# Graph attention on one core: one-hot matrices by ScalarE and VectorE instead of by matrix products, and another order of the gathers' holds

## The chip, the core and the metric

The kernel runs on one core of a Trainium2 chip. The metric is the device time of one execution in microseconds; a smaller one is better. Traces come from the hardware profiler, from one execution on the same core.

## The reference, cut to what matters

There are 6250 nodes of 128 features, 200000 edges sorted by destination (`dst`), with random sources (`src`) and 64 edge features, and 8 heads of 16.

```python
q = (x @ Wq + bq).reshape(N, 8, 16); k = ...Wk...; v = ...Wv...
scores = jnp.sum(q[dst] * k[src], axis=-1) * 16 ** -0.5 + (edge_attr @ We + be)
e = jnp.exp(scores - jax.ops.segment_max(scores, dst, N)[dst])
denom = jax.ops.segment_sum(e, dst, N) + 1e-10
agg = jax.ops.segment_sum((e / denom[dst])[:, :, None] * v[src], dst, N)
out = layernorm(x + agg.reshape(N, 128) @ Wo + bo)
```

All is float32. The number of nodes in a stretch of edges is small, since the edges are sorted: a half block of edges touches at most 64 nodes in a row.

## The kernel before, in words

**Tiling.** A tile is 128 edges. The edges are cut into 57 blocks (`b`). A full block has two halves of 14 tiles, 28 tiles; each half touches at most 64 nodes, so a block's 128 partitions hold 64 nodes of each half. A block is worked in 7 steps (`q`) of 4 tiles (2 pairs); 391 of the steps are full. The program is written out in full, without loops, as a list of slots (`v`): slot v works on step v, 7 slots a block. Each engine runs its own list in order and waits on semaphores.

**Prologue.** Rows of keys and values of all nodes are computed and stored as `kv_table` in device memory. The first block's are computed from gathered rows of x.

**A step.** GpSimd gathers the key and value rows of 4 tiles, one indirect DMA a tile (L523), into `kv_buf`, which holds three blocks. TensorE spreads the block's queries to edges: `spread_q` (L1230) multiplies a one-hot matrix (node by edge) with `q_blk` into one of two banks `ps_q`. VectorE multiplies with the keys (`multiply`, L850) and adds up by head (`dot`, L860). 12 slots later (SLOT + LAG) the weights are there; VectorE multiplies the values with them (`weigh`, L870) into one of two buffers `wv`, ScalarE copies the weights beside them (`copy_weights`, L655), and one slot after that TensorE adds them up by node with a one-hot matrix (edge by node): `sum_step` (L1266).

**One-hot matrices.** In slot v TensorE's `match(v)` (L1210, L1216) computes both matrices for later use: that by node of step v+1 and that by edge of step v-12, as products of bfloat16 codes. The code of an edge is made of its relative destination d, that of a node of its number n, so that the product is -(n-d)^2 or, for equal ones, 0. ScalarE's `copy_hots(v)` (L613, L617) takes relu(1 + product), which is 1 or 0, from the bank `ps_t` into one of two buffers `hots`. `match(v)` waits for the copy of slot v-1, `spread_q(v)` and `sum_step(v)` for that copy too, and `copy_hots(v)` for `match(v)`, the spread of v-1 and the sums of slot v-2. The edge codes are computed in the prologue by ScalarE from `dst_row`, stored to `code_table`, and loaded by block, 2 x 10.5 KB, by SP (`load_codes`).

**Once a block** TensorE also signals ten things: left-over row, maxima crossing edges, edge terms, edge terms turned, carried row summed, ends turned, new queries, halves folded, aggregate turned, rows times Wo. So it signals 7 + 7 + 7 + 10 = 31 times a full block. Of these, VectorE waits for the fold (`add_folded`), the left-over row (`scale_carry`), the ends turned (`crossing_maxima`, L930) and the crossing maxima (`edge_maxima`), and TensorE waits for VectorE's answers in the slots beside them.

**The order around the change.** In a slot TensorE's list is: spread, match, sums, then what is once a block. VectorE's is: weigh, multiply, the block's maxima, dot, the block's end. ScalarE's is: copy_hots, exponentials, copies for the block's end, copy_weights. SP's list is by block: edges of b+1 (1024 KB), x of b+3, codes of b+1, end distances of b+1, then the store of block b-3, for which it waits longest.

**The holds.** GpSimd could run far ahead. From block 6 on (`HELD`) step q's gathers are held to the work two steps behind (`AHEAD`):

```python
if b >= HELD and t == t0:     pool.wait_ge(s_byedge, q - AHEAD + 1)
if b >= HELD and t == t0 + 1: pool.wait_ge(s_matched, HOTS_TO[slot_of(q - AHEAD)])
if b >= HELD and t == t0 + 2: pool.wait_ge(s_summed, q - AHEAD - SLOT - LAG)
```

In full blocks these are TensorE's spread, match and sums of slot q-2, which it does in this order.

## Time and profile before

| what | us |
|---|---|
| median of 3 runs | 2431.14 |
| lowest, highest | 2421.57, 2438.39 |
| span of the profiled execution, its own time | 2449.4 |
| TensorE matmul busy | 1545.6 |
| VectorE busy | 1370.8 |
| ScalarE busy | 454.6 |
| GpSimd busy | 1496.0 |

The span goes from the first to the last instruction of one execution; the profile gives no other time of it. Busy times are the sums over an engine's instructions. Idle time of an engine is put down to what ended it; "issue" is idle time for which the profile shows no cause, "remote" is idle time ended by something it can't name. Ends of matmuls are modelled, not measured.

### The profile page before, as it was taken

The page shows a single profiled execution, that of the slowest core. Times are in us where ns is not written, and L with a number is a line of the kernel's source. Part 1 is how long each engine was busy: PE and PEld are TensorE (multiplying, and loading weights), DVE is VectorE, ACT ScalarE, POOL GpSimd, SP SyncE. Part 2 cuts the span into 40 slices and gives each one's busy share as a digit, 9 for nine tenths or more (in the row PEclk, how much of TensorE's full clock was granted, in tenths as well). Part 3 has the DMA queues.
Part 4 walks back from the last instruction along what each step waited for, and adds up shares of the span by engine and source line. Part 5 has one row for each costly group of instructions (what it writes and reads, how often), then busy time and mean ns, then how long its engine had stood idle before and what let it go on. Part 6 is the DMA issues. An engine that isn't in the chain of part 4 may idle for free.

```text
span 2449.4 us, 25231 instructions
## 1 busy us (share of the span) xinstructions
PE 1545.6 (63%) x6655; PEld 1051.5 (43%) x6655; DVE 1370.8 (56%) x3214; ACT 454.6 (19%) x1496; POOL 1496.0 (61%) x1572
## 2 busy tenths in 40 slices
PE   5354576657665757566656666566766666666566
PEld 4233454435343434444444444344444444444344
DVE  4254575656555655555655656555555555556556
ACT  1011121212121211111111212111211212111112
POOL 4736546666666666666666666666666666666661
PEclk7677788868778777877887887877878778788878
DMA  6423334343334334343434343434334343434331
GB/s 248 160 84 105 94 101 130 107 123 115 118 117 130 109 108 130 107 131 108 129 108 128 111 129 108 128 108 125 112 113 127 110 128 111 126 111 127 108 106 31
DMA packets 115143, 288.11 MB, mean 118 GB/s; under 512 B 45909, under 2 KB 53856, under 8 KB 107960
## 3 DMA queue, kind: packets, MB, share of 16 engines
q0 software_dynamic: 74624, 203.26, 28.3%
q1 hardware_dynamic: 37628, 76.52, 9.4%
q10 hardware_dynamic: 2748, 6.69, 0.7%
q8 instruction: 57, 0.93, 0.2%
q14 instruction: 86, 0.70, 0.1%
HBM read 274.69 MB, written 11.67 MB: 117 GB/s over the span
## 4 chain that ended last, share of the span: by engine, by line
PE 40%; issue 25%; another core or an unknown queue 14%; DVE 10%; POOL 9%; DMA 1%; ACT 1%; DVEq 0%; ACTq 0%; POOLq 0%
PE ps_q L1230 14%; PE ps_a L1266 11%; POOL kv_buf L523 9%; PE ps_e L1242 2%; PE ps_t L1216 2%; PE ps_t L1210 2%; DVE prod L850 1%; DVE score L860 1%; DMA kv_buf<-kv_table,src_i 1%; PE ps_s L1294 1%; DVE wv L870 1%; PE ps_a L1319 1%; DVE run_fwd L912 1%; PE ps_a L1320 1%
## 5 line engine op out<-in xcount | busy, mean ns | idle before, releaser
L523 POOL DMA_INDIRECT kv_buf<-kv_table,src_i x1536 | 1465.6, 954 | 899.6 <-issue 407.5
L1230 PE MATMUL ps_q<-q_blk,hots 128*128 128x256 f32 x1564 | 566.4, 497 | 553.8 <-issue 553.6
L1230 PEld LDWEIGHTS ps_q<-q_blk,hots 128*128 128x128 f32 x1564 | 351.9, 246 | 677.7 <-issue 625.2
L1266 PE MATMUL ps_a<-wv,hots 128*128 128x272 f32 x1564 | 559.9, 490 | 8.5 <-issue 5.6
L613 ACT ACTIVATE hots<-ps_t 128x512 f32<-128x512 f32 x377 | 225.1, 597 | 1784.8 <-remote 1035.1
L850 DVE TENSOR_TENSOR prod<-ps_q,kv_buf 128x512 f32<-128x512 f32 (+1 forms) x392 | 268.7, 685 | 497.8 <-remote 322.7
L870 DVE TENSOR_TENSOR wv<-kv_buf,ps_w 128x512 f32<-128x512 f32 (+1 forms) x392 | 266.3, 679 | 238.8 <-remote 179.5
L1266 PEld LDWEIGHTS ps_a<-wv,hots 128*128 128x128 f32 x1564 | 335.4, 238 | 61.0 <-issue 10.4
L860 DVE TENSOR_REDUCE score<-prod 128x32 f32<-128x512 f32 (+1 forms) x392 | 267.2, 682 | 7.9 <-issue 0.2
L930 DVE TENSOR_TENSOR_SCAN ps_s<-seq_far,seq_left,ps_s 8x512 f32<-8x512 f32 x57 | 72.7, 1275 | 188.0 <-remote 155.0
L1309 PE MATMUL ps_a<-sums_sb,carry_from 128*1 128x136 f32 x112 | 28.0, 342 | 195.2 <-DVE sums_sb L982 154.8
L1216 PE MATMUL ps_t<-node_code,codes 128*128 128x128 bf16 x782 | 127.7, 252 | 1.9 <-ACT hots L617 1.9
L1210 PE MATMUL ps_t<-codes,node_code 128*128 128x256 bf16 (+1 forms) x392 | 128.3, 327 | 0.0
L1216 PEld LDWEIGHTS ps_t<-node_code,codes 128*128 128x128 bf16 x782 | 90.3, 116 | 68.3 <-issue 36.3
L1309 PEld LDWEIGHTS ps_a<-sums_sb,carry_from 128*1 128x1 f32 x112 | 4.8, 81 | 215.4 <-DVE sums_sb L982 170.0
L655 ACT COPY wv<-weight 128x32 f32<-128x32 f32 (+1 forms) x392 | 96.1, 245 | 1.3
L1319 PE MATMUL ps_a<-bias_row,ones 1*128 1x128 f32 x114 | 30.8, 354 | 76.6 <-ACT agg_t L663 75.3
L1210 PEld LDWEIGHTS ps_t<-codes,node_code 128*128 128x128 bf16 x392 | 45.3, 116 | 68.5 <-issue 52.9
L936 DVE TENSOR_TENSOR_SCAN seq_b<-seq_far,ps_s 8x512 f32<-8x512 f32 x57 | 68.3, 1198 | 0.0
L1242 PE MATMUL ps_e<-edge_f,w_e 128*32 128x512 f32 (+1 forms) x456 | 66.7, 660 | 0.0
L1319 PEld LDWEIGHTS ps_a<-bias_row,ones 1*128 1x128 f32 x114 | 18.7, 204 | 99.4 <-ACT agg_t L663 90.8
L982 DVE TENSOR_TENSOR sums_sb<-ps_a,sums_sb 1x136 f32<-1x136 f32 x57 | 16.9, 297 | 63.2 <-remote 60.2
(157 smaller groups left out, 1398.1 us busy)
## 6 DMA issues: line engine op xcount, KB each, us to landing
edge_f<-in_edge_blk SPq DMA_DIRECT2D x55, 1024.0 KB
kv_buf<-kv_table,src_i POOLq DMA_INDIRECT x1536
kv_table<-kv_buf ACTq DMA_DIRECT2D x12, 512.0 KB, 3.2
xt_blk<-in_x_t SPq DMA_DIRECT2D x114, 32.0 KB
out<-y_out SPq DMA_DIRECT2D x114, 32.0 KB
kv_buf<-in_x_perm SPq DMA_DIRECT2D x5, 512.0 KB
codes<-code_table SPq DMA_DIRECT2D x108, 10.5 KB
code_table<-kv_buf SPq DMA_DIRECT2D x1, 1344.0 KB
```

What stands on the lines that cost most here:

```text
L523: pool.indirect_dma_start(kv_buf[:, b % NBUF, t, :], None, kv_table, bass.IndirectOffsetOnAxis(ap=src_i[:, column:column + 1], axis=0)).th ...
L613: one = act.activation(hots[:, v % 2, :, :].rearrange("p k n -> p (k n)"), ps_t[:, :], ACT.Relu, bias=1.0)
L655: act.copy(wv[:, q % 2, 0:t1 - t0, D:WV], by_head(weight[:, b % 2, :], TILES[b])[:, :, t0:t1].rearrange("p h t -> p t h")).then_inc(s_besi ...
L850: dve.tensor_tensor(prod[:, q % 2, 0:n * D].rearrange("p (t d) -> p t d", d=D), ps_q[q % 2][:, 0:n * D].rearrange("p (t d) -> p t d", d=D) ...
L860: dve.tensor_reduce(score[:, b % 2, :, t0:t1].rearrange("p h t -> p t h"), prod[:, q % 2, 0:(t1 - t0) * D].rearrange("p (t h d) -> p t h d ...
L870: dve.tensor_tensor(wv[:, q % 2, 0:t1 - t0, 0:D].rearrange("p t (h d) -> p t h d", d=HD), kv_buf[:, b % NBUF, t0:t1, D:KV].rearrange("p t ...
L1210: one = pe.matmul(ps_t[:, 0:(t1 - t0) * W], node_code[:, :], codes[:, b % CBUF, t0 * W:t1 * W], start=True, stop=True)
L1216: one = pe.matmul(ps_t[:, QUAD * W + k * P:QUAD * W + (k + 1) * P], codes[:, b % CBUF, t0 * W + k * P:t0 * W + (k + 1) * P], node_code[:, ...
L1230: one = pe.matmul(ps_q[q % 2][:, k * 2 * D:(k + 1) * 2 * D], hots[:, (v - 1) % 2, 0, k * P:(k + 1) * P], q_blk[:, b % QBUF, :], start=True ...
L1242: one = pe.matmul(ps_e[at:at + P // EGROUPS, 0:n * P].rearrange("k (s p) -> k s p", p=P), w_e2[:, :], edge_f[:, b % 2, :].rearrange("k (s ...
L1266: one = pe.matmul(sums(b), hots[:, (v - 1) % 2, 1, k * P:(k + 1) * P], wv[:, q % 2, 2 * k:2 * k + 2, :].rearrange("p j w -> p (j w)"), sta ...
L1319: pe.matmul(projected(b), ones[0:1, :], bias_row[:, QKV:QKV + D], start=True, stop=False)
```

## The change

`match`, the codes, their table and their set-up go. The matrices come from elsewhere:

- By node, on ScalarE: SP loads the destinations of block b+1 as int32, each half's row repeated over 64 partitions (`load_dst`, 2 x 448 KB a block, two buffers). In slot v ScalarE computes |d - n| for step v+3 (`gaps_to_nodes`) and relu(1 - that) for step v+2 (`hots_by_node`), each 128x256, into four buffers.
- By edge, on VectorE: `hots_by_edge` compares the numbers 0 to 63 with each edge's relative destination, 128x256, ahead of `weigh`, into three buffers.
- `ps_t` becomes a third bank for the spread (`SPREADS`); `wv` has three buffers.
- The gathers from block 6 on wait for other signals. The wait for `weigh` of three blocks before stays only before block 6.

```diff
+    NHOT, NGAP, EHOT, WVBUF, SPREADS = 4, 3, 3, 3, 3
...
-            def load_codes(b):
-                if b >= CBUF:
-                    last = (b - CBUF) * SLOT + GS[b - CBUF] - 1
-                    sync.wait_ge(s_matched, HOTS_TO[last + SLOT + LAG])
+            def load_dst(b):
+                if b >= DBUF:
+                    sync.wait_ge(s_gap, FIRST[b - DBUF + 1])
                 n = HALF[b] * P
                 for j in range(2):
                     row = 2 * b + j
+                    sync.dma_start(dst_bc[j * W:(j + 1) * W, b % DBUF, 0:n], dst_row[row:row + 1, 0:n].to_broadcast([W, n])
+                                   ).then_inc(s_dstbc[b % DBUF], 16)
...
-                    if b >= NBUF:
+                    if NBUF <= b < HELD:
                         pool.wait_ge(s_weighted, steps_over(b - NBUF, t1))
...
                         if b >= HELD and t == t0:
+                            pool.wait_ge(s_summed, q - AHEAD - SLOT - LAG)
+                        if b >= HELD and t == t0 + 1:
                             pool.wait_ge(s_byedge, q - AHEAD + 1)
-                        if b >= HELD and t == t0 + 1:
-                            pool.wait_ge(s_matched, HOTS_TO[slot_of(q - AHEAD)])
-                        if b >= HELD and t == t0 + 2:
-                            pool.wait_ge(s_summed, q - AHEAD - SLOT - LAG)
...
+            def gaps_to_nodes(q):
+                b, g = STEPS[q]
+                t0, t1 = STEP[b][g]
+                if g == 0:
+                    act.wait_ge(s_dstbc[b % DBUF], 32 * (b // DBUF + 1))
+                if q >= NGAP:
+                    act.wait_ge(s_near, q - NGAP + 1)
+                act.activation(gaps[:, q % NGAP, 0:(t1 - t0) * W], dst_bc[:, b % DBUF, t0 * W:t1 * W], ACT.Abs,
+                               bias=neg_node[:, b:b + 1]).then_inc(s_gap, 1)
+
+            def hots_by_node(q):
+                b, g = STEPS[q]
+                t0, t1 = STEP[b][g]
+                act.wait_ge(s_gap, q + 1)
+                if q >= NHOT:
+                    act.wait_ge(s_byedge, q - NHOT + 1)
+                act.activation(near_hots[:, q % NHOT, 0:(t1 - t0) * W], gaps[:, q % NGAP, 0:(t1 - t0) * W], ACT.Relu,
+                               bias=1.0, scale=-1.0).then_inc(s_near, 1)
...
-                copy_hots(-1)
-                for v in SLOTS:
-                    if v in HOTS_TO:
-                        copy_hots(v)
+                act.wait_ge(s_node, NODE["of blocks"])
+                for v in range(-3, SLOTS[-1]):
+                    if step_in(v + 3) is not None:
+                        gaps_to_nodes(step_in(v + 3))
+                    if step_in(v + 2) is not None:
+                        hots_by_node(step_in(v + 2))
...
-            dve.memset(codes[:, :, :].rearrange("p i e -> p (i e)").bitcast(F32), ONES_BF16).then_inc(s_const, 1)
...
+            def hots_by_edge(q):
+                b, g = STEPS[q]
+                t0, t1 = STEP[b][g]
+                pairs = (t1 - t0) // 2
+                if q >= EHOT:
+                    dve.wait_ge(s_summed, q - EHOT + 1)
+                dve.tensor_tensor(
+                    edge_hots[:, q % EHOT, 0:pairs * P].rearrange("p (k j n) -> p k j n", j=2, n=W),
+                    iota_n[:, 0:W].rearrange("p (a b n) -> p a b n", a=1, b=1).to_broadcast([P, pairs, 2, W]),
+                    rel[:, columns(b, 0, TILES[b])].rearrange("p (j t a) -> p t j a", j=2, a=1)[:, t0 // 2:t1 // 2]
+                    .to_broadcast([P, pairs, 2, W]), ALU.is_equal)
...
                     if step_in(v - SLOT - LAG) is not None:
+                        hots_by_edge(step_in(v - SLOT - LAG))
                         weigh(step_in(v - SLOT - LAG))
...
-            def match(v):
...
             def spread_q(v):
                 pe.wait_ge(s_qcopied, b + 1)
-                pe.wait_ge(s_copied, HOTS_TO[v - 1])
-                if q >= 2:
-                    pe.wait_ge(s_product, q - 1)
+                pe.wait_ge(s_near, q + 1)
+                if q >= SPREADS:
+                    pe.wait_ge(s_product, q - SPREADS + 1)
...
-                    if v in HOTS_TO:
-                        match(v)
```

`weigh` and `copy_weights` now wait for the sums of three steps before where it was two, and `sum_step` reads `edge_hots` and the third `wv`.

## Rows read from the trace of the kernel before

**Rows 1.** The page, busy time, share of the span and instructions of each engine.
```profile
PE 1545.6 (63%) x6655; PEld 1051.5 (43%) x6655; DVE 1370.8 (56%) x3214; ACT 454.6 (19%) x1496; POOL 1496.0 (61%) x1572
```

**Rows 2.** Stretches: length; busy us (records) of PE, PEld, DVE, ACT, POOL; clock, DMA share, GB/s.
```profile
283.00:352.00 69.00, 47.46 (x232) 33.38 (x230) 48.77 (x113) 15.78 (x52) 29.55 (x31) 0.84 0.31 93
1057.00:2349.00 1292.00, 830.96 (x3566) 562.25 (x3566) 733.13 (x1708) 243.42 (x807) 827.22 (x868) 0.79 0.39 117
```

**Rows 3.** Groups by line, 1057 to 2349 us, GpSimd: busy, mean ns, idle before.
```profile
L523 POOL DMA_INDIRECT kv_buf<-kv_table,src_i x868 | 828.0, 954 | 465.1 <-issue 229.4 <-remote 168.9 <-PE ps_q L1230 50.5
```

**Rows 4.** Timeline, 1196.5 to 1207.4 us: start, length, engine, line, [idle before].
```profile
1197.62 0.28 PE L1216 MATMUL ps_t<-node_code,codes 128*128 128x128 bf16 x2
...
1197.73 1.14 PE L1266 MATMUL ps_a<-wv,hots 128*128 128x272 f32 x4
...
1203.44 0.95 POOL L523 DMA_INDIRECT kv_buf<-kv_table,src_i  x1 [0.30 <-issue]
...
1206.66 0.60 ACT L613 ACTIVATE hots<-ps_t 128x512 f32<-128x512 f32 x1 [10.69 <-remote]
1206.80 0.69 DVE L870 TENSOR_TENSOR wv<-kv_buf,ps_w 128x512 f32<-128x512 f32 x1 [2.76 <-remote]
1206.89 0.95 POOL L523 DMA_INDIRECT kv_buf<-kv_table,src_i  x1 [2.51 <-remote]
...
1207.35 0.77 PE L1230 MATMUL ps_q<-q_blk,hots 128*128 128x256 f32 x1 [8.49 <-issue]
```

**Rows 5.** Waits, 1057 to 2349 us: who, for what: us, times, longest.
```profile
ACT hots L613 <- remote: 636.8, 82, 13.2
...
PE ps_q L1230 <- issue: 310.7, 69, 10.7
ACT hots L613 <- PE ps_t L1216: 253.4, 88, 8.5
...
DVE prod L850 <- remote: 190.5, 52, 8.5
POOL kv_buf L523 <- remote: 168.9, 86, 3.2
...
DVE ps_s L930 <- remote: 101.6, 19, 8.8
...
POOL kv_buf L523 <- PE ps_q L1230: 50.5, 52, 2.7
...
POOL kv_buf L523 <- PE ps_a L1266: 11.8, 11, 2.3
```

**Rows 6.** Groups by line, whole span, from L613 on with forms kept apart.
```profile
L1210 PE MATMUL ps_t<-codes,node_code 128*128 128x256 bf16 (+1 forms) x392 | 128.3, 327 | 0.0
L1216 PE MATMUL ps_t<-node_code,codes 128*128 128x128 bf16 x782 | 127.7, 252 | 1.9 <-ACT hots L617 1.9
...
L613 ACT ACTIVATE hots<-ps_t 128x512 f32<-128x512 f32 x377 | 225.1, 597 | 1784.8 <-remote 1035.1 <-PE ps_t L1216 499.3 <-issue 219.1
L617 ACT ACTIVATE hots<-ps_t 128x256 f32<-128x256 f32 x26 | 9.9, 383 | 76.8 <-issue 29.6 <-PE ps_t L1210 18.2 <-remote 15.1
L584 ACT ACTIVATE kv_buf<-kv_buf,run_max 128x1792 bf16<-128x1792 int32 x1 | 1.8, 1788 | 0.0
...
L850 DVE TENSOR_TENSOR prod<-ps_q,kv_buf 128x512 f32<-128x512 f32 x390 | 267.8, 687 | 497.6 <-remote 322.7 <-PE ps_q L1230 110.2 <-issue 60.4
...
L736 DVE MEMSET codes<- 128x3584 f32 x1 | 3.0, 3045 | 0.7 <-issue 0.7
```

**Rows 7.** The chain of waits, 1270 to 1292 us: start, length, what.
```profile
1287.28 2.51 DMA kv_buf<-kv_table,src_i
```

**Rows 8.** A stretch with an edge load, columns as in rows 2.
```profile
1208.00:1213.00 5.00, 3.60 (x13) 2.18 (x11) 3.43 (x9) 0.73 (x2) 3.94 (x4) 0.73 0.89 311
```

**Rows 9.** One line's instructions: shortest, median, longest ns, first and last start.
```profile
L523 POOL DMA_INDIRECT kv_buf<-kv_table,src_i x1536: 941/947/1846, 63.8 to 2404.8; - x192
...
L957 DVE TENSOR_TENSOR run_max<-run_max,cand x57: 242/391/455, 165.8 to 2427.5; 128x224 f32<-128x224 f32 x54, 128x208 f32<-128x208 f32 x1, 128x128 f32<-128x128 f32 x1, 128x80 f32<-128x80 f32 x1
```

More of the change, by code:

```diff
@@ L89, in graph_attention @@
     FIRST_HALVES = [(g, h) for g in range(GS[0]) for h in range(2)]
-    assert all(t1 - t0 == QUAD for t0, t1 in STEP[0]) and NB >= 4 and len(GROUPS) >= KNOWN
+    assert all(t1 - t0 == QUAD for t0, t1 in STEP[0]) and NB >= 4
     HALVES_TO = [sum(1 for j, _ in HALVES if j < k) for k in range(len(GROUPS) + 1)]
@@ L275, in graph_attention @@
         SETUP = numbered("ident zero", "iotas", "ident")
-        s_rowcode = sem("s_rowcode")
-        ROWCODE = numbered("less", "rel", "middle", "squares")
-        s_nodecode = sem("s_nodecode")
-        NODECODE = numbered("numbers", "squares", "high", "columns", "rows")
+        s_node = sem("s_node")
+        NODE = numbered("numbers", "of blocks")
         s_const = sem("s_const")
-        CONST = numbered("ones", "zeros", "codes", "iota", "bias kv", "scaled")
+        CONST = numbered("ones", "zeros", "iota", "bias kv", "scaled")
         s_win = sem("s_win")
@@ L429, in _ @@
                 load_x(b)
-            sync.wait_ge(s_const, CONST["codes"])
-            sync.wait_ge(s_codetable, 16)
-            load_codes(0)
+            load_dst(0)
             for i in range(STAGES):
@@ L474, in _ @@
                     if b + 1 < NB:
-                        load_codes(b + 1)
+                        load_dst(b + 1)
                         load_seq(b + 1)
@@ L727, in _ @@
             dve.memset(eps_c[:, :], LN_EPS)
-            for k, less in enumerate((0.0, -32.0, -16.0)):
-                dve.memset(less_c[:, k:k + 1], less)
             dve.memset(q_blk[:, :, :], 0.0)
@@ L796, in _ @@
             dve.tensor_copy(base_bc[:, :], base_ps).then_inc(s_win, 1)
+            dve.wait_ge(s_node, NODE["numbers"])
+            for j in range(2):
+                own = slice(j * W, (j + 1) * W)
+                one = dve.tensor_scalar(neg_node[own, :], base_ps[own, j::2], -1.0, neg_n[own, :], ALU.mult, ALU.add)
+            one.then_inc(s_node, 1)
             dve.tensor_scalar(carry_from[:, 1::2], step_ps[:, 1::2], part[:, 0:1], None, ALU.is_equal)
@@ L1265, in sum_step @@
                 for k in range((t1 - t0) // 2):
-                    one = pe.matmul(sums(b), hots[:, (v - 1) % 2, 1, k * P:(k + 1) * P],
-                                    wv[:, q % 2, 2 * k:2 * k + 2, :].rearrange("p j w -> p (j w)"),
+                    one = pe.matmul(sums(b), edge_hots[:, q % EHOT, k * P:(k + 1) * P],
+                                    wv[:, q % WVBUF, 2 * k:2 * k + 2, :].rearrange("p j w -> p (j w)"),
                                     start=(t0 + k == 0), stop=False)
@@ L1326, in _ @@
                     project_q(b)
-                match(-1)
                 for v in SLOTS:
```

170 lines of the change are left out of this document (36 added, 134 removed).

## The prediction

> **What bounds the kernel now.** I read the shares first: no engine is full. TensorE is busy 63% of the span, GpSimd 61%, VectorE 56%, ScalarE 19% [rows 1]. So the bound is a wait or a ring of waits, and the stretch view says where. In 1057 to 2349 us, 868 gathers were issued, 31 blocks of 28, so a block takes 1292 / 31 = 41.7 us. The earlier stretch 283 to 352 us holds 232 matmul records against 3566 / 31 = 115 a block, two blocks in 69 us, while GpSimd was busy 29.6 us of it [rows 2]. TensorE, ScalarE and VectorE can thus do a block in 34.5 us when GpSimd issues little.
>
> GpSimd's own floor: a gather takes 0.954 us [rows 3] and the next starts 0.30 us later [rows 4], so 28 take 28 x 1.255 = 35.1 us. The block is 6.6 us longer. GpSimd's waits in the stretch say why: 168.9 us end by something unnamed, 50.5 by the spread, 11.8 by the sums, 231 us in 149 pauses, 4.8 a block; without the 0.30 us that stands before any gather it is 186 us, 6.0 a block [rows 5]. GpSimd waits for TensorE.
>
> Why TensorE is late is the point of the case. The records of the matching and sum matmuls end at 1197.9 and 1198.9, yet ScalarE, VectorE and GpSimd, which all wait for exactly these, go on at 1206.66, 1206.80 and 1206.89: three engines released within 0.25 us, eight us later, and 2.3 us after the last of an unbroken row of gathers [rows 4]. ScalarE's copy then releases the next spread at 1207.35, where TensorE had shown 8.49 us of "issue". I read it so: **while gathers are issued back to back, what TensorE finishes is seen late; when GpSimd runs out of leave, all of it comes at once.** The trace doesn't say whether the matmuls or their signals are held.
>
> That makes a ring of signals cost what work does not. Before, spread(v) needs the copy of the hots of v, which needs the matching product of slot v-1, which is behind spread(v-1): one slot per seen signal. In the stretch ScalarE idles 636.8 + 253.4 us before that copy, TensorE 310.7 us before the spread, VectorE 190.5 us before its multiply [rows 5].
>
> **The change, part by part.**
> *Products out.* 391 slots lose one 128x256 and two 128x128 bf16 products, 128.3 + 127.7 = 256 us of TensorE's busy time [rows 6], and 7 of its 31 signals a block (7 spread, 7 matched, 7 summed, 10 once a block). It leaves 24 against 28 gathers. As TensorE is not full, the 256 us are worth nothing as work; what counts is the ring. After, spread(v) needs a hot that ScalarE made two slots before, out of loaded numbers, and the product of v-3; the sum in slot v needs VectorE to be past multiply(v-2). So after one seen signal TensorE can go on for two slots, not one.
> *ScalarE.* It loses a 597 ns copy and gets two operations on 256 columns. The 256-column copy took 383 ns, the 1792-column one from int32 1788 [rows 6]; I take 0.4 us each, 0.8 for 0.6, +80 us busy, to 22%. Cover: it works two and three slots ahead. If that goes (a load of destinations late in slot 4, where the first gap of the next block stands ahead of the exponentials), the sums are late next.
> *VectorE.* 391 comparisons, 128x256. Between 391 ns at 224 columns [rows 9] and 687 at 512 [rows 6] lie 1.03 ns a column, so 0.425 us, 166 us in all: 3.0 us a block on 23.7 (733.1 / 31 [rows 2]). They stand before weigh and multiply. Covered in the slots where VectorE waits for TensorE or gathers anyway; naked in the two slots a block where fold, left-over row and turned ends go back and forth. So 0 to 166 us; I take 2 x 0.425 x 54 = 45 us.
> *Banks.* The freed bank lets spread run three ahead; a third wv buffer lets weigh and the weights' copy wait for sums one step older. No cost; in the gain of the ring.
> *Holds.* In slot v TensorE does spread, then sums, and signals in this order. The first gather of step v+2 used to go with spread(v), the second with the match, the rest with the sums. Now all four wait for the sums, and the second's wait for the spread is always met already: one wait, not two. Behind it only gathers queue. Cost: the first gather starts later by one to two signals. The landing after a last gather took 2.51 us [rows 7], so the data of step v+2 is there 5.0 + 2.5 = 7.5 us after the sums of v, and is wanted two slots, 10 us or more, later. Bounds: 0, or one pause a step (below). I take 0.
> *Loads.* Codes of 2 x 10.5 KB a block are replaced by 2 x 448 KB of destinations spread over partitions. The nearest row is the edge load of 1024 KB: in the 5 us around it the DMA engines are 0.89 busy [rows 8], against 0.39 on the whole [rows 2], 2.5 us more than usual. So 0 to 2.2 us a block, 126 us if every burst delayed a gather that is waited for; I take 0, since the edge burst didn't stop GpSimd (3.94 of 5 us busy) and these loads are issued four slots before their use. SP's queue: load_dst stands where load_codes stood, behind load_x, and its wait is over a slot or more before.
> *Set-up.* The code rows, their store and a memset of 3.0 us [rows 6] go: 0 to 6 us; I take 3.
>
> **The sum.** Between nothing and all of the 6.6 us I take half, 3.3: the ring's reach doubles, so a pause is needed half as often for it, while the ten block signals stay. 51 held blocks x 3.3 = 168; 168 - 45 + 3 = 126 us less. Against the profiled span of 2449.4, 2323. That span stands 18 us above the median of the runs, 2431.1, so **2305**.
>
> **A rule against the change.** The edge comparison is a two-input operation out of SBUF, issued while gathers run. The trace has such: a 224-column one of VectorE has a median of 391 and at most 455 ns, and over 1536 gathers the shortest is 941 and the median 947 [rows 9]. So neither holds the other by any amount that shows, and by these rows the comparison costs GpSimd nothing. The Trainium skill (SBUF — State Buffer, "Who interferes with whom") says that a VectorE instruction with two SBUF inputs contends with a GpSimd instruction that reads SBUF, and that whoever is first holds the other off wholly; by that rule the sum would be that of rival (e), 2471.
>
> **Rivals.**
> (a) *Floor reached*: the pauses vanish and GpSimd issues without a break: 2449 - 51 x 6.6 - 18 = 2095. For it: the 34.5 us of rows 2 and fewer signals than gathers. Against it: those two blocks had a half-idle GpSimd; the ten block signals still go round.
> (b) *Nothing moves*: the turned ends (101.6 us of waiting [rows 5]) and the other once-a-block exchanges take what the ring gives back: 2431, within 1%.
> (c) *Slower, a pause a step.* Place: GpSimd before a step's first gather. With the leave given in one piece after the sums, every step may run into a pause; the unnamed ones took 168.9 / 86 = 1.96 us, 1.66 without the gap. Seven a block make 35.1 + 11.6 = 46.7 us, 5.0 more: 2431 + 255 = 2686. It decides from 6.0 / 1.66 = 3.6 such pauses a block upward. For it: GpSimd can no longer slip one gather per signal. Against it: sums now come second, not third, behind fewer signals.
> (d) *Slower, the comparison in VectorE's path*, with no gain beside it: 2431 + 166 = 2597. Against it: VectorE idles 18 of 41.7 us a block.
> (e) *Slower, gathers held*: each of the 391 comparisons holds a gather for its own 0.425 us. GpSimd's floor grows by 3.0 us a block, 166 in all: 2305 + 166 = 2471. Against it: rows 9.
>
> **Chances.** Forecast 0.46, its own range 2200 to 2400; (a) 0.13; (b) 0.13; (c) 0.13; (d) 0.09; (e) 0.06. A measurement here tells about 1% from no change. Faster 0.59, same 0.13, slower 0.28. Leaving out the fast half of (a) and most of (c), the range is 2140 to 2590.
>
> **What would show it.** Right: the mean time of a block in the steady stretch near 38.5 us, GpSimd's waits for TensorE near 3 us a block, TensorE's idle time before spreads well under 310.7 us, VectorE 27 us busy a block, gathers still 0.95 us. Wrong: pauses before a step's first gather in most steps (c); GpSimd waiting while VectorE shows no idle time (d); gathers over 1 us (e); ScalarE waiting for loaded destinations. It fails if TensorE's results are late for another reason than gathers, so that two slots of reach pass no faster than one.

## The result, and the profile after

| kernel | median us | lowest, highest | runs |
|---|---|---|---|
| before | 2430.14 | 2421.57, 2438.39 | 4 |
| changed | 2401.8 | 2400.68, 2406.15 | 4 |

The ratio is 0.9886, with a 95% interval of 0.9862 to 0.991: 28 us faster, where 126 were forecast. The direction was right and the time is inside the whole range of the forecast (2140 to 2590), just outside the 2200 to 2400 that the forecast gave its own case; the size was off by a factor of four and a half. The profiled execution of before has a span 19 us above its median, the changed one's 2398.6 us is at its own. So the two spans differ by 50.8 us and the medians by 28.

The page of the changed kernel, busy time of the engines, which answers to [rows 1]:

```profile
PE 1449.8 (60%) x5480; PEld 979.4 (41%) x5480; DVE 1493.1 (62%) x3591; ACT 526.8 (22%) x1868; POOL 1496.5 (62%) x1572
```

TensorE's busy time fell by 96 us, not by the 256 of the removed groups [rows 6]. The modelled spans of matmuls overlap: in the trace of before, the removed groups have only 55 of the 1545.6 us to themselves. So a group's busy time is more than what its removal takes off the engine.

The same stretch as in [rows 2], 1057 to 2349 us, columns as there:

```profile
1057.00:2349.00 1292.00, 782.07 (x2992) 524.30 (x2993) 829.87 (x2000) 292.40 (x1046) 848.39 (x888) 0.76 0.51 141
```

888 gathers for 868: 28 x 1292 / 888 = 40.7 us a block for 41.7. VectorE works 829.9 / 31.7 = 26.2 us a block, close to the 27 forecast. Groups by line of that stretch (first row) and of the whole span (the others), to be held against [rows 3, 6]:

```profile
L487 POOL DMA_INDIRECT kv_buf<-kv_table,src_i x888 | 848.4, 955 | 445.6 <-issue 252.3 <-remote 149.4 <-PE ps_a L1191 38.8
...
L559 ACT ACTIVATE x_first<-dst_bc,neg_node 128x256 f32<-128x256 int32 (+1 forms) x392 | 197.0, 503 | 47.8 <-DMA dst_bc<-in_dst_row 30.4 <-issue 17.3
L807 DVE TENSOR_TENSOR x_first<-iota_n,rel 128x256 f32<-128x256 f32 (+1 forms) x392 | 162.4, 414 | 0.0
L568 ACT ACTIVATE x_first<-x_first 128x256 f32<-128x256 f32 (+1 forms) x392 | 157.8, 403 | 215.8 <-remote 193.4 <-PE ps_q L1156 8.9 <-PE ps_t L1156 8.1
```

A gather is as long as before, 0.955 us. The comparison takes 0.414 us (0.425 taken), ScalarE's two operations 0.503 and 0.403 (0.4 each taken). GpSimd's wait for something unnamed is 149.4 us where it was 168.9, 5.0 us are left of the wait for the spread (50.5 before), and that for the sums went from 11.8 to 38.8.

The waits of the stretch, longest groups, to be held against [rows 5]:

```profile
...
DVE prod L787 <- remote: 210.5, 40, 8.8
...
PE ps_a L1191 <- ACT wv L605: 96.8, 25, 10.8
...
PE ps_a L1204 <- DVE sums_sb L926: 91.8, 16, 8.3
PE ps_a L1234 <- issue: 82.9, 19, 5.7
```

TensorE no longer waits before the spread (310.7 us before). It waits before the sums, 182 us for 2, and before the fold (L1204) and the left-over row (L1234), two once-a-block exchanges with VectorE: 281 us, 8.9 a block, where it waited 93 us, 3.0 a block, before. The same picture as in [rows 4], from the timeline of the changed kernel (start, length, engine, line, idle time before):

```profile
1212.89 1.33 PE L1156 MATMUL ps_q<-q_blk,x_first 128*128 128x256 f32 x4
...
1214.06 1.08 PE L1191 MATMUL ps_a<-wv,x_first 128*128 128x272 f32 x4
...
1216.12 0.95 POOL L487 DMA_INDIRECT kv_buf<-kv_table,src_i  x1 [0.30 <-issue]
1217.89 0.69 DVE L787 TENSOR_TENSOR prod<-ps_q,kv_buf 128x512 f32<-128x512 f32 x1 [6.57 <-remote]
1217.95 0.42 ACT L568 ACTIVATE x_first<-x_first 128x256 f32<-128x256 f32 x1 [6.26 <-remote]
```

The sums end at 1215.1, the row of gathers at 1217.07, and VectorE and ScalarE go on 0.06 us apart at 1217.9, as three engines did before.

**Where the pauses went.** From all gaps between gathers over 0.45 us between 434 and 2300 us (0.30 of each taken off, as the usual gap), sorted by the slot of the step that the gather is held to:

| | gathers | pauses a block | us a block | of it slots 0, 3, 4, 5 | slots 1, 2, 6 | gathers in a row |
|---|---|---|---|---|---|---|
| before | 1255 | 4.15 | 6.41 | 2.66 | 3.75 | 6.7 |
| changed | 1282 | 2.64 | 5.51 | 0.26 | 5.25 | 10.6 |
| before with the changed holds | 1267 | 3.20 | 6.05 | 2.53 | 3.52 | 8.7 |
| changed with holds like the earlier ones | 1253 | 3.53 | 6.14 | 4.42 | 1.72 | 7.9 |

The last two rows are of experiments below. The slots are parted by what the first two rows show. In TensorE's list the sums of slots 1, 2 and 6 come next after once-a-block work: the fold and the left-over row (1), the turned ends and aggregate (2), the carried row and the new queries (6). But slot 3, which has the crossing maxima at its head, lost its pauses (1.31 to 0.09 us a block).

So the pauses of the other slots did vanish (2.4 us a block), and 1.5 of it came back in slots 1, 2 and 6, in fewer and longer pauses; with the holds alike (third row against second) it is 2.3 and 1.7. Where a pause stands also depends on the hold: with the first gather held to the spread, most of them stand in slots 0 and 3, so the split says where GpSimd waits and not by itself why. What remains is 0.9 us a block, 46 us over 51 blocks in this pair of profiles, less 6 us at the end: from the end of the last gather to the end of the span it is 49.7 us for 43.6. Ten comparisons of 0.414 us, 4.1 in all, start in that time; whether they lengthen it is not shown.

### The profile page after: what moved, and what is told of

The parts are those of the page before. It is cut to its first block, busy times and chain, and to the rows that moved or that the text cites. A ratio compares the mean times of both kernels' runs of the same rounds, so it can differ in the third digit from the quotient of the medians.

```text
span 2398.6 us, 23254 instructions
## 1 busy us (share of the span) xinstructions
PE 1449.8 (60%) x5480; PEld 979.4 (41%) x5480; DVE 1493.1 (62%) x3591; ACT 526.8 (22%) x1868; POOL 1496.5 (62%) x1572
## 4 chain that ended last, share of the span: by engine, by line
POOL 32%; another core or an unknown queue 21%; issue 19%; PE 17%; DVE 9%; ACT 2%; DMA 1%; ACTq 0%; DVEq 0%
POOL kv_buf L487 32%; PE ps_a L1191 5%; PE ps_q L1156 4%; DVE prod L787 2%; DVE wv L819 2%; PE ps_t L1156 2%; PE ps_e L1168 1%; DVE score L797 1%; PE ps_a L1234 1%; DVE x_first L807 1%; ACT x_first L559 1%; PE ps_s L1213 1%; DMA kv_buf<-kv_table,src_i 1%; PE ps_s L1219 0%
## 5 line engine op out<-in xcount | busy, mean ns | idle before, releaser
L1191 PE MATMUL ps_a<-wv,x_first 128*128 128x272 f32 x1564 | 571.8, 500 | 325.3 <-ACT wv L605 188.5
L1191 PEld LDWEIGHTS ps_a<-wv,x_first 128*128 128x128 f32 x1564 | 362.3, 242 | 497.1 <-issue 212.1
L787 DVE TENSOR_TENSOR prod<-ps_q,kv_buf 128x512 f32<-128x512 f32 x262 | 179.9, 686 | 472.2 <-remote 296.2
L1156 PE MATMUL ps_q<-q_blk,x_first 128*128 128x256 f32 x1046 | 354.7, 472 | 22.6 <-issue 22.6
L1156 PEld LDWEIGHTS ps_q<-q_blk,x_first 128*128 128x128 f32 x1046 | 234.6, 239 | 79.1 <-issue 40.7
L559 ACT ACTIVATE x_first<-dst_bc,neg_node 128x256 f32<-128x256 int32 (+1 forms) x392 | 197.0, 503 | 47.8 <-DMA dst_bc<-in_dst_row 30.4
L568 ACT ACTIVATE x_first<-x_first 128x256 f32<-128x256 f32 (+1 forms) x392 | 157.8, 403 | 215.8 <-remote 193.4
L1234 PE MATMUL ps_a<-sums_sb,carry_from 128*1 128x136 f32 x112 | 33.7, 402 | 249.5 <-issue 134.2
L1156 PE MATMUL ps_t<-q_blk,x_first 128*128 128x256 f32 x518 | 179.9, 481 | 4.8 <-DVE prod L787 4.3
L613 ACT COPY agg_t<-ps_a 128x128 f32<-128x128 f32 x57 | 15.1, 265 | 672.8 <-issue 266.5
L807 DVE TENSOR_TENSOR x_first<-iota_n,rel 128x256 f32<-128x256 f32 (+1 forms) x392 | 162.4, 414 | 0.0
L1204 PE MATMUL ps_a<-sums_sb,carry_from 64*1 64x136 f32 x114 | 30.9, 365 | 189.8 <-DVE sums_sb L926 141.7
L879 DVE TENSOR_TENSOR_SCAN ps_s<-seq_far,seq_left,ps_s 8x512 f32<-8x512 f32 x57 | 72.6, 1274 | 103.2 <-remote 58.7
L1156 PEld LDWEIGHTS ps_t<-q_blk,x_first 128*128 128x128 f32 x518 | 118.7, 244 | 34.1 <-issue 14.2
L1234 PEld LDWEIGHTS ps_a<-sums_sb,carry_from 128*1 128x1 f32 x112 | 4.8, 81 | 275.3 <-issue 149.2
L1204 PEld LDWEIGHTS ps_a<-sums_sb,carry_from 64*1 64x1 f32 x114 | 4.6, 77 | 219.5 <-DVE sums_sb L926 157.5
L595 ACT ACTIVATE ps_w<-run_fwd 128x112 f32<-128x112 f32 (+3 forms) x114 | 29.4, 258 | 244.8 <-issue 227.2
```

The source lines that it names most:

```text
L559: act.activation(gaps[:, q % NGAP, 0:(t1 - t0) * W], dst_bc[:, b % DBUF, t0 * W:t1 * W], ACT.Abs, bias=neg_node[:, b:b + 1]).then_inc(s_ga ...
L568: act.activation(near_hots[:, q % NHOT, 0:(t1 - t0) * W], gaps[:, q % NGAP, 0:(t1 - t0) * W], ACT.Relu, bias=1.0, scale=-1.0).then_inc(s_n ...
L787: dve.tensor_tensor(prod[:, q % 2, 0:n * D].rearrange("p (t d) -> p t d", d=D), ps_q[q % SPREADS][:, 0:n * D].rearrange("p (t d) -> p t d" ...
L807: dve.tensor_tensor(edge_hots[:, q % EHOT, 0:pairs * P].rearrange("p (k j n) -> p k j n", j=2, n=W), iota_n[:, 0:W].rearrange("p (a b n) - ...
L879: dve.tensor_tensor_scan(turned_ends, far[:, 0:SEQ], turned_ends, left, ALU.add, ALU.max).then_inc(s_seqf, 1)
L1156: one = pe.matmul(ps_q[q % SPREADS][:, k * 2 * D:(k + 1) * 2 * D], near_hots[:, q % NHOT, k * P:(k + 1) * P], q_blk[:, b % QBUF, :], start ...
```

## Two kinds of chips

The experiments met a surprise that belongs ahead of them. The kernel before takes 2430.14, 2433.39, 2431.96 and 2426.88 us on four occasions, and 2022.74, 2021.14 and 2022.43 us on three others. The first are called late chips here, the second prompt chips. No chip on record was used on two occasions, so the chip and the occasion can't be told apart; all comparisons are with the kernel before on the same chip. On a prompt chip both kernels were profiled too. GpSimd's gathers over the whole span, before (first fence) and changed (second):

```profile
L523 POOL DMA_INDIRECT kv_buf<-kv_table,src_i x1536 | 1460.5, 951 | 474.4 <-issue 424.0 <-PE ps_q L1230 38.9 <-DVE wv L870 5.2
```

```profile
L487 POOL DMA_INDIRECT kv_buf<-kv_table,src_i x1536 | 1471.4, 958 | 489.2 <-issue 441.4 <-PE ps_a L1191 30.6 <-PE ps_t L1156 7.9
```

The gather is as long as on the late chip (951 against 954 ns in [rows 3]), and there is no unnamed wait at all. The timeline of the kernel before on the prompt chip, against [rows 4]:

```profile
1201.97 0.28 PE L1216 MATMUL ps_t<-node_code,codes 128*128 128x128 bf16 x2
...
1202.21 0.94 POOL L523 DMA_INDIRECT kv_buf<-kv_table,src_i  x1 [0.30 <-PE ps_q L1230]
...
1202.28 0.60 ACT L613 ACTIVATE hots<-ps_t 128x512 f32<-128x512 f32 x1 [2.19 <-PE ps_t L1216]
```

ScalarE starts 0.03 us after the matching product's end, in the middle of a row of gathers. The trace also records when a semaphore is raised. Each raise on record is set here against the last matmul that raises it and had ended by then (434 to 2300 us; 434 to 1900 on the prompt chip; 434 to 1600 without gathers):

| | late: sums, mean us | late: spread, mean us |
|---|---|---|
| before, late chip | 2.7 | 1.8 |
| changed, late chip | 2.6 | 3.0 |
| before, prompt chip | 0.01 | 0.01 |
| changed, prompt chip | 0.01 | 0.01 |
| changed without gathers, late chip | 0.01 | 0.01 |

TensorE's signals are late only while gathers run and only on late chips. Of these two signals, 70% (before) and 87% (changed) of the raises that are more than 0.3 us late fall into a pause of the gathers, half of those 2.0 and 2.7 us or more after the last gather's end: they come in bursts.

Three things limit this. Raises are missing from the traces of late chips: 251 are there for 314 sums in before's window, 221 for 322 in the changed kernel's, 169 for 314 dot products of VectorE in before's; on the prompt chip each of these is there. The means are of the recorded ones. No run separates the issuing of gathers from their transfers, since without gathers both are gone. And every execution on record was profiled, so that no run shows whether the recording itself, whose records go missing on the same chips, takes part in the lateness. What differs between the chips no run shows.

## The experiments

Letters of theories are explained in each expectation. Each ratio has its 95% interval behind it.

### The new holds and the new matrices, one without the other

The kernel before with the changed holds:

```diff
-                    if b >= NBUF:
+                    q = FIRST[b] + g
+                    if NBUF <= b < HELD:
                         pool.wait_ge(s_weighted, steps_over(b - NBUF, t1))
...
                         if b >= HELD and t == t0:
+                            pool.wait_ge(s_summed, q - AHEAD - SLOT - LAG)
+                        if b >= HELD and t == t0 + 1:
                             pool.wait_ge(s_byedge, q - AHEAD + 1)
-                        if b >= HELD and t == t0 + 1:
-                            pool.wait_ge(s_matched, HOTS_TO[slot_of(q - AHEAD)])
-                        if b >= HELD and t == t0 + 2:
-                            pool.wait_ge(s_summed, q - AHEAD - SLOT - LAG)
```

> The kernel before with nothing but the changed kernel's holds: all four gathers of a held step wait for the sums two steps before. Theory H: pauses of 2.4 us in place of 1.8, 4.3 a block: 2.6 us a block more, 2560 us. Theory V and theory X: the order of the holds does little, 2430 within 20; then the whole of the 28 us comes from the matrices. If it is below 2415, the holds alone brought the gain.

Measured on a prompt chip, for which nothing was forecast: 2035.62 us, 1.006 (1.0039 to 1.0081). Again, for a late chip:

> The kernel before with the changed kernel's holds, once more; where before takes 2021 to 2023 it took 2036. Where before takes about 2430: theory H (the holds gave the gain: one pause for each step instead of three waits): 2395 to 2410. Theory V (the matrices made ahead gave it): 2430 or more, since the sums are still behind the matching product. The matching ring with the later leave: 2560 (from my first expectation).

Measured: 2430.37 us for 2431.96, 0.9996 (0.9963 to 1.0029). On a late chip the holds alone give nothing, and the 2560 of my first expectation was far off. The changed kernel with holds like the earlier ones. There is no match to hold the second gather to, so it waits for nothing of its own:

```diff
-                    if NBUF <= b < HELD:
+                    if b >= NBUF:
                         pool.wait_ge(s_weighted, steps_over(b - NBUF, t1))
...
                         if b >= HELD and t == t0:
+                            pool.wait_ge(s_byedge, q - AHEAD + 1)
+                        if b >= HELD and t == t0 + 2:
                             pool.wait_ge(s_summed, q - AHEAD - SLOT - LAG)
-                        if b >= HELD and t == t0 + 1:
-                            pool.wait_ge(s_byedge, q - AHEAD + 1)
```

> The changed kernel with the holds spread first: a held step's first gather waits for the spread two steps before, its third for the sums (and, as in the kernel before, every step for the weighing of three blocks before, which is long past). Theory H (the gain was eaten by holding all four gathers to the sums, which makes each of GpSimd's 2.6 pauses a block 2.4 us long where the kernel before had 4.3 of 1.8): the pauses get shorter by about 0.6 us, 1.6 us a block, 80 us in all: 2320 us. Theory V (the gain was eaten by VectorE's comparison): no change, 2402 within 10. Theory X (what remains are the exchanges between TensorE and VectorE once a block, at which GpSimd pauses whatever it waits for): 2395 to 2415.

Measured on a prompt chip, again without a forecast for it: 2036.12 us, 1.0067 (1.0048 to 1.0086). Again:

> The changed kernel with the earlier holds (the first gather for the spread, the third for the sums), once more; where signals are seen at once it took 2036, 13 less than the changed kernel. Where before takes about 2430: theory V (the matrices alone give the gain): 2385 to 2410. Rival H (they give it only with the new holds): 2425 to 2440.

Measured on a late chip: 2443.67 us for 2426.88, 1.0053 (1.0023 to 1.0082), just above rival H's range; theory V falls. So on late chips the matrices alone cost 0.5%, the holds alone nothing, and the two together gain 1.1%. GpSimd's waits from 1057 to 2349 us in this kernel:

```profile
POOL kv_buf L487 <- remote: 111.5, 56, 3.4
POOL kv_buf L487 <- PE ps_q L1156: 77.6, 47, 2.6
POOL kv_buf L487 <- PE ps_t L1156: 38.9, 23, 2.7
```

The wait for the spread, 5.0 us in the changed kernel, is back with 117 us (`ps_t` is the third bank of the spread). By the table's measure the pauses are 6.14 us a block for 5.51, and the mean gather is 965 ns for 956, 13 us in all. The forecast had put the holds at nothing.

### What holds are worth at all

The changed kernel with no holds from block 6 on but the wait for `weigh` of three blocks before; and with holds to the sums three steps behind:

```diff
-    HELD, AHEAD = 6, 2
+    HELD, AHEAD = 6, 3
```

> The gathers from block 6 on wait for nothing but the buffer, for weigh of three blocks before, as in the first blocks. Where before takes about 2021 us, theory P (the pause once a block before a step's first gather, 0.36 us a block, is the new hold's): no pause, 2030 to 2038, as with the spread first (2036). Rival: the gathers are then further ahead and VectorE and TensorE are the bound in places: 2045 or more. Where before takes about 2430, theory L (late signals while gathers run): GpSimd runs ahead for up to three blocks, then stalls for a block's end; TensorE sees less of its chances, 2400 to 2500. Rival (the holds' pauses cause the loss): 2100 to 2300.

Prompt chip: 2035.03 us, 1.0058 (1.0041 to 1.0076).

> The changed kernel without holds from block 6 on, once more; where signals are seen at once it took 2035. Where before takes about 2430: theory L (the holds cut the rows of gathers, and signals are seen in the cuts): rows of 28 and more gathers, 2410 to 2500. Rival (the holds cost what they save): 2370 to 2400.

Late chip: 2717.54 us, 1.1188 (1.1122 to 1.1254), far beyond both expectations. GpSimd's waits there, 1057 to 2349 us:

```profile
POOL kv_buf L483 <- DVE wv L815: 338.0, 62, 9.8
```

GpSimd runs until the buffers are full and then stands, waiting for `weigh`, some two times a block, 5.5 us each (62 times in 770 / 28 = 27.5 blocks). Holds that cut the rows of gathers are worth the difference between 1.1188 and 0.9886 there, and less than nothing on a prompt chip, 1.0058 against 1.0114. That agrees with lateness under gathers in a row; the forecasts had its direction and not its size.

> The changed kernel with the gathers held to the sums three steps behind, not two. Where signals are seen at once: the pause once a block goes (0.36 us a block), 2030 to 2040. Where before takes about 2430: theory L: GpSimd has 16 gathers in a row where it had 12, the pauses are fewer and longer, the time the same within 1%, 2385 to 2425. Rival (the hold itself costs the pauses): excess under 4 us a block, under 2340.

Late chip: 2399.4 us, 0.9854 (0.9817 to 0.989), as the changed kernel, as theory L had it, though the rows of gathers were no longer (9.9 in the mean). The holds' distance isn't what sets the pauses.

### Banks and buffers

```diff
-    NHOT, NGAP, EHOT, WVBUF, SPREADS = 4, 3, 3, 3, 3
+    NHOT, NGAP, EHOT, WVBUF, SPREADS = 4, 3, 3, 2, 2
```

> The changed kernel with two spread banks and two wv buffers, as before, the rest as changed. Where signals are seen at once (before 2021 us) the third ones hide nothing: 2040 to 2055, as the changed kernel. Where they are late (before about 2430), theory V (the reach of the ring gave the gain): 2430 or more, the 28 us are lost again; rival H (the matrices made ahead gave it, banks and buffers nothing): 2402.

Late chip: 2395.9 us, 0.9848 (0.979 to 0.9907). The third spread bank and the third `wv`, which the forecast counted into the ring's reach, give nothing. The matrices by node stay two slots ahead in this run; no run took only that away.

### The number of TensorE's signals

```diff
+                    if k == 0 and t1 - t0 > 2:
+                        one.then_inc(s_idle, 1)
                 one.then_inc(s_byedge, 1)
```

and the same in the sums.

> The changed kernel in which TensorE also signals after the first of the two products of each spread and of each sum, to a semaphore that nobody waits for: 38 signals a block instead of 24, and no more work. Theory S (signals of TensorE are what gathers hold up, about one gets through a gather): 10 signals a block more than gathers can pass; each adds up to 1.25 us: +3 to +12 us a block, 2550 us or more. Theory M (TensorE's matmuls themselves are held up while gathers are issued, or the number of signals doesn't matter): no change, 2402 within 10.

Prompt chip, without a forecast for it: 2047.76 us, 1.0113 (1.0072 to 1.0154), against 1.0114 for the unaltered changed kernel.

> The changed kernel with 14 more signals of TensorE a block that nobody waits for, 38 for 24, once more; where signals are seen at once it took 2048, as the changed kernel. Where before takes about 2430: theory S (while gathers run about one signal is seen for each gather, so the number of signals sets how late they are): 2440 or more, up to 2550. Rival M (the number doesn't count, only how far TensorE may go on after one seen signal): 2390 to 2415.

Late chip: 2409.01 us, 0.9898 (0.9857 to 0.9938), against 0.9886 (0.9862 to 0.991). Fourteen more signals a block cost nothing that shows: theory S falls, and with it "24 signals against 28 gathers" as a reason.

### The comparison

In the changed kernel a second, unused comparison beside the first; in the kernel before, one unused comparison ahead of each `weigh`, of which this is a part:

```diff
+                    dve.tensor_tensor(
+                        unused[:, q % 3, 0:pairs * P].rearrange("p (k j n) -> p k j n", j=2, n=W),
...
+                        .to_broadcast([P, pairs, 2, W]), ALU.is_equal)
```

> The changed kernel with each edge comparison made twice, the second into a buffer that nobody reads: 162 us more on VectorE. Theory V (the comparison is in the path and ate the gain): +120 to +162 us, 2520 to 2565. Theory H and X: covered but in the slots of the exchanges, +45 us by the prediction's term (2 of 7 slots): 2447. If the comparison is wholly covered: 2402 within 10. If comparisons hold gathers: a gather's mean time rises from 956 ns and GpSimd's busy time by up to 160 us.

Prompt chip, where only the last of the forecasts applies: 2079.95 us, 1.0279 (1.0255 to 1.0302). The gathers' row there:

```profile
L487 POOL DMA_INDIRECT kv_buf<-kv_table,src_i x1536 | 1502.3, 978 | 484.7 <-issue 446.2 <-PE ps_a L1196 21.5 <-PE ps_t L1161 8.1
```

Against the changed kernel on a prompt chip, busy 1471.4: 30.9 us more, as much as the 31 us between 2048.9 and 2080 (33 by the two ratios, since these are two chips). VectorE's own 162 us more are hidden; the longer gathers are not.

> The kernel before with the comparison added ahead of each weigh from block 1 on, 385 times, its output unused: only VectorE's extra work and what it does to the gathers. Theory G (the comparison lengthens the gathers beside it, at GpSimd's floor the only thing that counts): where before takes 2021 us, gathers 957 to 960 ns, the time 2030 to 2042; VectorE's own 160 us stay hidden. Rival D (VectorE's work doesn't touch the gathers): 951 ns and 2018 to 2026. Where before takes about 2430: 2470 to 2560.

Late chip: 2437.64 us for 2433.39, 1.0028 (1.0002 to 1.0053). Gathers there:

```profile
L524 POOL DMA_INDIRECT kv_buf<-kv_table,src_i x1536 | 1475.8, 961 | 870.5 <-issue 408.9 <-remote 248.1 <-PE ps_q L1243 94.7
```

10.2 us more than in the kernel before, whose gathers were busy 1465.6 us over its span (954 ns each, as in [rows 3]), and the time is 4 us longer, far under the 2470 to 2560 expected. So the comparison's whole price in the kernel before on a late chip is 4 us, at most 13, where the forecast had 45. In the changed kernel it was not measured on a late chip.

### The loads of destinations

The loads and ScalarE's wait for them left out from block 2 on:

```diff
+                if b >= DBUF:
+                    return
                 for j in range(2):
                     row = 2 * b + j
...
-                if g == 0:
-                    act.wait_ge(s_dstbc[b % DBUF], 32 * (b // DBUF + 1))
+                if g == 0 and b < DBUF:
+                    act.wait_ge(s_dstbc[b % DBUF], 32)
```

> Leaves out the loads of destinations from block 2 on (the matrices by node are then those of other blocks). Where before takes about 2021 us, the changed kernel takes 2049, with gathers of 958 ns against 951, 11 us. Theory G (the comparison on VectorE lengthens the gathers; the loads cost nothing): gathers stay at 957 to 959 ns, the time at 2040 to 2052. Rival D (the loads do it, 47 MB more traffic): gathers back to 951 ns, the time 2030 to 2040. Where before takes about 2430: G 2395 to 2405; D 2350 to 2385.

Prompt chip: 2035.71 us, 1.0055 (1.0033 to 1.0076). The gathers:

```profile
L489 POOL DMA_INDIRECT kv_buf<-kv_table,src_i x1536 | 1471.0, 958 | 475.4 <-issue 450.9 <-PE ps_a L1193 9.6 <-PE ps_t L1158 6.1
```

The gathers stay at 958 ns, so theory G holds for their length; but the time falls by 13 us, as in D, through GpSimd's idle time, 475.4 us for 489.2: the wait for the sums is 9.6 us for 30.6. With the loads the changed kernel has 10 gaps over 0.45 us between gathers from 434 to 1900 us, 0.36 us a block, all before a step's first gather; without them it has none. Taking either away, the loads or the new hold, gives the same 13 us (2035.7; 2036.1 and 2035.0).

### Both kernels on one prompt chip, with and without gathers

> The changed kernel, unaltered, beside the kernel before, to have both on one chip (the first experiments ran on a chip where the kernel before takes 2023 us, not 2430). Theory F: where TensorE's signals are seen in time, the kernel before is at GpSimd's floor (57 x 35.1 = 2001 us and the start), so the change has nothing to give there: ratio 1.00 to 1.01 where before takes about 2023; 0.985 to 0.992 where before takes about 2430. Rival R: the shorter ring of waits is worth its 28 us on every chip: ratio 0.986 on both.

Measured: 2048.92 us for 2021.14, 1.0114 (1.0088 to 1.014). The changed kernel is slower there, by a little more than theory F allowed; rival R falls.

> The kernel before, unaltered, for its trace on this chip. Theory L (the chips differ in how late TensorE's signals are seen while gathers run): where the time is about 2023, the delay between the records of the sums and their being seen is under 1 us and GpSimd's unnamed waits are under 1 us a block; where it is about 2430, 2.7 us in the mean as in the trace shown first. Rival K: the chips differ in the length of a gather: 0.954 us and 0.30 us between two on the one, under 0.85 in all on the other.

Measured: 2021.5 us. Theory L holds. No gap over 0.45 us stands between the gathers from 434 to 1900 us: GpSimd is at its floor, 28 x (0.949 + 0.305) = 35.1 us a block (757.4 us busy, 243.1 idle for 798 gathers in 1000 us).

> The same with the kernel before: the gathers left out from block 6 on. 33 to 36 us a block (34.5 in the two blocks in which GpSimd was half idle), 1850 to 2000 us. Theory R (the matching product lengthens the ring of waits): 3 us a block or more above the changed kernel without gathers. Rival: both are bound by VectorE's work and the exchanges once a block, and the changed kernel, which has 3 us a block more on VectorE, is 1 to 3 us a block slower.

> Leaves out the gathers from block 6 on (keys and values are then those of earlier blocks). It shows how fast TensorE, VectorE and ScalarE are by themselves. Theory L (gathers make TensorE's signals late): no signal is seen late, a block takes VectorE's busy time, 27 us, and the waits between engines; 28 to 33 us a block, 1500 to 1850 us in all, on either chip. Rival (e): without gathers the comparison gets shorter too, 0.414 to under 0.40 us. Rival: the lateness has nothing to do with gathers, and on a chip where before takes 2430 a block stays over 38 us.

Measured: 1638.58 us, 0.81 (0.8079 to 0.8121), and 1658.28 us, 0.8197 (0.8174 to 0.8221); the first is far under the 1850 to 2000 expected, the second is in its range. Busy times from 500 to 1500 us, columns as in [rows 2], before (first) and changed:

```profile
500.00:1500.00 1000.00, 843.51 (x4212) 585.23 (x4213) 850.63 (x2010) 287.79 (x946) 0.00 (x0) 0.87 0.14 46
```

```profile
500.00:1500.00 1000.00, 804.62 (x3402) 571.34 (x3402) 924.50 (x2248) 333.29 (x1188) 0.00 (x0) 0.87 0.28 78
```

By the starts of a once-a-block instruction of VectorE, a block takes 27.3 us before and 27.6 changed. Both are VectorE's, 92% busy in the changed kernel. The ring with the matching product costs nothing where signals are prompt: theory R falls. And the comparison takes 415 ns with gathers and 414 without.

> The changed kernel without gathers from block 6 on, once more, for a chip where before takes about 2430 us; where it took 2021, this took 1658. Theory L (the gathers make TensorE's signals late): no signal is late after block 6, and the time is 1658 and the 60 us that the first blocks lose, 1700 to 1740. Rival M (the lateness has another source on that chip): signals of TensorE stay 1 us or more late in the mean, the time over 1850.

Measured on a late chip: 1762.62 us, 0.7237 (0.7203 to 0.727), over the 1740 expected and far under rival M's 1850. Of the 108 us by which its profiled span is longer than on the prompt chip 100 come early, while there are gathers: the 7th scan for the crossing maxima (L879, one a block) starts at 361.1 us for 260.7, the 57th at 1732.8 for 1625.0. After that no signal is late, and the stretch is the same to a tenth of a per cent:

```profile
500.00:1500.00 1000.00, 807.67 (x3421) 575.07 (x3420) 924.75 (x2244) 336.15 (x1195) 0.00 (x0) 0.87 0.28 79
```

## Why the prediction was right in direction and wrong in size

**The bound, right.** GpSimd's floor of 35.1 us a block and the reading of the unnamed waits as late signals of TensorE under gathers in a row are both borne out: the floor by the prompt chips, the lateness by the kernel without gathers on a late chip. The floor bounds the kernel before only on prompt chips. The 34.5 us that the forecast gave the other engines came from a stretch in which signals were still late at times; by themselves they take 27.3.

**Products out, the mis-sized term.** The forecast put half of the 6.6 us, 168 us, on "the ring's reach doubles". Measured: 0.9 us a block, 46 us in the pair of profiles, with the new holds; with holds like the earlier ones the same products out cost 0.5%, 13 us. The step failed in two places. First, the reach by banks and buffers gave nothing (without them 2395.9 us), nor did the lower count of signals (with 14 more 2409.0). Second, most of the saving came back elsewhere: with the holds alike, slots 0, 3, 4 and 5 lost 2.3 us of pauses a block, and slots 1, 2 and 6 gained 1.7. TensorE's waiting before the spread went, 310.7 us, and its waiting before the fold and the left-over row rose from 93 to 281 us, that before the sums from 2 to 182. That is rival (b)'s mechanism, the once-a-block exchanges, and the forecast had a row for it (the turned ends, 101.6 us of waiting [rows 5]) but gave it nothing within its own sum. That the exchanges take back what the other slots save is read from where the pauses and waits stand, and is not shown; no run took an exchange away. The right direction is thus in part luck: the reach alone did not give it.

**Holds, wrong at nothing.** With the new matrices, holds like the earlier ones give 1.0053 and the new ones 0.9886, 1.7% or 41 us apart; with the old matrices, it is 1 and 0.9996. The gain of the change on late chips exists only with both. The forecast took the moved wait for neutral. With the earlier kind of holds the changed kernel waits 117 us for the spread, with the new ones 5; why the new order gives nothing while a matching product stands before the sums is left open. Rival (c), a pause in every step at 2686, didn't come: 2.64 pauses a block, under the 3.6 from which it decides.

**VectorE, over-sized.** The comparison's length was right (0.414 for 0.425), its place on the path wrong: 4 us (0.5 to 13) for 45, in the kernel before. Rival (d) falls. On a prompt chip, where GpSimd is at its floor, its time on VectorE is hidden.

**The rule against the change.** Gathers did get longer beside comparisons: 951 to 958 ns on prompt chips with the first comparison and 978 with a second, 954 to 961 in the kernel before on a late chip. Rival (e) wanted 3.0 us a block, 166 in all; the first comparison costs 10 to 11 us in all in these two cases and the second 31. In the changed kernel on a late chip the gathers are only 3.3 us longer in all, with holds like the earlier ones 16. By the Trainium skill (SBUF — State Buffer, "Who interferes with whom") whoever is first holds the other off wholly; the runs show a fraction of that, 0.03 us of gather time for each first comparison and 0.08 for each added one of 0.414 us, and none on the comparison's side (415 ns with gathers, 414 without). The same section of the Trainium skill infers that a `tensor_tensor`, as the comparison is one, does not hold up the writing of DMA descriptors; the comparison alone makes the gathers of the kernel before 10 us longer in all. So the size that the runs show for this pair of instructions lies between the two statements.

**Loads, wrong at nothing on prompt chips.** 13 us, by a longer wait for the sums. On late chips it wasn't tried.

**ScalarE, set-up.** 0.91 us a step for 0.8; from 1057 to 2349 us its full-sized |d - n| waited 13.8 us for the loads of destinations. The 3 us of the set-up can't be told from the spread of the runs.

**The sum on late chips, in the pair of profiles:** pauses -46; the first 141 gathers done 9 us earlier; the end +6; gathers +1; together -48 of -50.8. The 9 us are probably not the change's: counting the 28 gathers of x, the kernel before reached the 141st at 255 us in its profile, two others with the same start at 244 and 247, and the changed one at 246. So 9 of the 19 us by which the profiled execution of before stands over its median are in its start; the other 10 are not located. The medians' 28 is the result.

**On prompt chips** the change is worth +28 us: gathers +8 (+11, and -3 for the 28 gathers of x in the first block, 26.6 us for 29.4), idle time between them +15 (13 of it hold and loads together), the end +5.5 (51.4 us from the end of the last gather for 45.9). It can't gain there: GpSimd is at 35.1 us, the others at 27.

No kernel tried beats both everywhere. On late chips the changed kernel with two banks (0.9848, 0.979 to 0.9907) or with `AHEAD` 3 (0.9854, 0.9817 to 0.989) is as good as the changed one (0.9886, 0.9862 to 0.991). On prompt chips the kernel before is the fastest.

## What to carry to other kernels

When one engine's results are released in bursts beside another engine's unbroken row of instructions, a longer ring of waits may not be what to mend first: ask where the bursts fall and which once-a-block exchange stands near each, since here most of what the other slots saved was waited for again beside them. A moved hold is priced together with the list of the engine it waits for, never as neutral. And a wait that the profile can't name is worth measuring on a second chip, before a kernel is changed for it.

## What was not expected of the hardware

The same program takes 2430 us on some chips and 2021 on others, 17% less, with gathers of 954 and 951 ns. What differs in the traces is TensorE's signals, 2.7 us late in the mean against 0.01, and 0.01 on a late chip too once gathers stop. The spans of before differ by 428 us; 69 stand ahead of the 141st gather, and GpSimd's pauses of 6.4 us a block in 51 blocks are 327 more. The signals of VectorE and ScalarE that are on record are 0.01 to 0.04 us late in the mean on late chips; a quarter to over a half of them are missing there. The changed kernel without holds takes 12% more than before on a late chip and 0.6% more on a prompt one. On a late chip TensorE's granted clock is lower as well, 0.786 against 0.838 for the kernel before, with more idle time before its matmuls; without gathers it is 0.87 on both.
